# The second layer of an expert block with the weights stationary instead of the tokens

## The reference, cut to what matters

```python
def _expert_mlp(x, W1, b1, W2, b2, W3, b3):
    h = jax.nn.gelu(jnp.einsum('bnd,dh->bnh', x, W1) + b1, approximate=False)
    h = jax.nn.gelu(jnp.einsum('bnh,hk->bnk', h, W2) + b2, approximate=False)
    return jnp.einsum('bnh,hd->bnd', h, W3) + b3
...
_, topk_idx = jax.lax.top_k(scores, TOP_K)
for i in range(num_expert):
    w = jnp.mean((topk_idx == i).astype(x.dtype), axis=-1, keepdims=True)
    outputs = outputs + _expert_mlp(x, W1[i], b1[i], W2[i], b2[i], W3[i], b3[i]) * w
```

## Time and profile before

| | us |
|---|---|
| median of 3 runs | 420.71 |
| lowest and highest | 419.45, 421.0 |
| span of the profiled execution | 431.4 |

### The profile page before, as it was taken

How to read it: one execution, slowest core, us unless ns; L and a number is a source line. 1 busy time by engine, 2 the same in 40 slices (tenths; PEclk the granted TensorE clock), 3 DMA queues, 4 the chain that set the end, 5 groups by cost and what they waited for, 6 DMA issues and landing times.

```text
span 431.4 us, 7928 instructions
## 1 busy us (share of the span) xinstructions
PE 311.5 (72%) x2495; PEld 190.2 (44%) x2495; DVE 271.2 (63%) x709; ACT 183.2 (42%) x406; POOL 163.2 (38%) x185
## 2 busy tenths in 40 slices
PE   1757599999876748544999999999925275786820
PEld 1553244444343213343566666666515243564710
DVE  3587768888857233569777677767665854544513
ACT  7340147766434663402444454455382206335602
POOL 8203004134311999768055222322330472054560
PEclk9966989999998858655999999999985775696975
DMA  5689913434110456411356111010002013111114
GB/s 191 230 211 277 403 72 92 138 92 140 52 49 5 153 186 196 140 44 57 97 183 210 33 33 26 27 32 21 14 21 97 25 50 84 36 47 37 32 40 147
DMA packets 23237, 43.31 MB, mean 100 GB/s; under 512 B 3661, under 2 KB 13612, under 8 KB 23070
## 3 DMA queue, kind: packets, MB, share of 16 engines
q0 software_dynamic: 8336, 26.47, 18.9%
q1 hardware_dynamic: 13758, 13.64, 11.8%
q10 hardware_dynamic: 1104, 2.70, 1.8%
HBM read 27.25 MB, written 15.30 MB: 99 GB/s over the span
## 4 chain that ended last, share of the span: by engine, by line
PE 51%; DVE 20%; issue 8%; DMA 7%; POOL 5%; ACT 5%; another core or an unknown queue 1%; SPq 1%; ACTq 1%; POOLq 0%; DVEq 0%
PE pair L1115 14%; PE bank L1239 4%; PE bank L1012 4%; PE bank L1125 3%; PE bank L1136 3%; PE pair L970 3%; PE pair L1103 3%; DVE mA L1427 3%; PE bank L990 3%; POOL w_sb L663 2%; DMA back<-y_rows 2%; PE pair L1227 2%; POOL y_rows L733 2%; DMA y_rows<-y_sb,id_now 2%; PE bank L1004 2%
## 5 line engine op out<-in xcount | busy, mean ns | idle before, releaser
L1115 PE MATMUL pair<-w_sb,h 128*128 x276 | 64.7, 385 | 6.2 <-DVE h L1550 6.2
L1427 DVE TENSOR_REDUCE mA<-pair 128x2 f32<-128x256 f32 (+3 forms) x64 | 50.8, 821 | 16.6 <-PE pair L972 15.8
L820 ACT ACTIVATE h<-pair,cols 128x128 f32<-128x128 f32 x92 | 26.2, 368 | 79.2 <-PE pair L1103 55.9
L808 ACT ACTIVATE p_ring<-bank 128x512 f32<-128x512 f32 (+1 forms) x88 | 45.4, 563 | 32.6 <-PE bank L993 32.6
L656 POOL DMA_DIRECT2D w_ring<-in_L_ffn_W_dram x24 | 18.3, 765 | 97.4 <-DVE w_sb L1368 76.3
L717 POOL DMA_INDIRECT y_rows<-y_sb,id_now x21 | 25.0, 1190 | 70.5 <-DVE y_sb L1571 68.0
L990 PE MATMUL bank<-qr,kr 128*128 128x512 bf16 (+3 forms) x128 | 36.3, 328 | 8.8 <-ACT p_ring L808 8.6
L684 POOL DMA_INDIRECT x_slots<-sent,slot x32 | 31.8, 994 | 28.6 <-DVE slot L1670 17.1
L1115 PEld LDWEIGHTS pair<-w_sb,h 128*128 128x128 f16 x276 | 25.8, 99 | 36.3 <-issue 8.4
L970 PE MATMUL pair<-kr,qr 128*128 128x128 bf16 (+3 forms) x128 | 33.7, 320 | 7.2 <-DVE mA L1427 6.2
L820 ACT ACTIVATE h<-bank,cols 128x128 f32<-128x128 f32 x92 | 26.6, 392 | 7.2 <-PE bank L1125 7.2
(11 more groups left out here) (298 smaller groups left out, 653.2 us busy)
## 6 DMA issues: line engine op xcount, KB each, us to landing
w_ring<-in_L_ffn_W_dram POOLq DMA_DIRECT2D x24, 512.0 KB, 4.5
x_slots<-w_sb POOLq DMA_DIRECT2D x2, 2064.0 KB, 19.9
fc_sb<-in_L_ffn_c_fc_dram POOLq DMA_DIRECT2D x4, 512.0 KB
cp_sb<-in_L_ffn_c_proj_dram POOLq DMA_DIRECT2D x4, 512.0 KB
back<-y_rows SPq DMA_DIRECT2D x8, 256.0 KB, 3.3
kr<-k_rows SPq DMA_DIRECT2D x8, 204.0 KB
qr<-q_rows SPq DMA_DIRECT2D x8, 192.0 KB
x_slots<-w_sb ACTq DMA_DIRECT2D x1, 1290.0 KB, 7.2
```

The source lines that it names most:

```text
L808: act.activation(p_ring[:, w % P_RING, 0:width], bank(4 + v % 3)[:, 0:width], ACT.Exp).then_inc(exp_done, 1)
L820: ins = act.activation(to[:, c * P:(c + 1) * P], got[:, c * P:(c + 1) * P], ACT.Gelu, bias=cols[:, bass.ds(e * HC + (bias_row + c), 1)], s ...
L1115: ins = mm(bank(3), h1[:, s, hq, k * P:(k + 1) * P], w2_sb[k][wq][:, bass.ds(e * HID, HID)], start=(k == 0 and n == 0), stop=(k == HC - 1 ...
L1427: dve.tensor_reduce(mA[:, b, t, g * G + 2 * hp:g * G + 2 * hp + 2], got[:, :, 0:(t + 1) * P], AX_X, ALU.max).then_inc(a_used, 1)
```

## The change

The second layer takes the weights as the stationary operand and the activations as the moving one: for each of 4 groups of 128 output units, 4 x 3 matmuls of 128 columns. Its result has hidden units on the partitions, so Gelu reads it from PSUM at once. copy_z, transpose_z, the tile `z32` and the semaphores `z_copied` and `tz_done` go away. The result alternates between banks 3 and 4, and the second layer waits for gelu2 of two blocks before. On ACT gelu2(i) now stands ahead of gelu1(i+2); on DVE the order is the table, split_2(i), result(i-1), copy_x(i+3), split_1(i+2).

```diff
@@ -830,10 +829,10 @@
 
             def gelu2(i, e):
                 s = i % 2
-                act.wait_ge(tz_done, i + 1)
+                act.wait_ge(mm2_done, i + 1)
                 if i >= 1:
                     act.wait_ge(h2_ready, i)
-                hidden_units(i, e, bank(4), h32[:, 1], ROW_B2, gelu2_done)
+                hidden_units(i, e, bank(3 + s), h32[:, 1], ROW_B2, gelu2_done)
 
             act.activation(warm[:, 1:2], ident[:, 0:1], ACT.Gelu)
             act.wait_ge(a_used, len(a_order))
@@ -842,11 +841,11 @@
             act.wait_ge(tab_ready, 1)
             of = list(table(mybir.EngineType.Activation, 0, 0, LEAD + 2))
             for i in range(NB):
+                gelu2(i, of[i])
                 if i + 2 < NB:
                     gelu1(i + 2, of[i + 2])
                 if i + 3 < NB and i + 3 >= len(of):
                     of += table(mybir.EngineType.Activation, 0, i + 3, 1)
-                gelu2(i, of[i])
 
 
             act.wait_ge(l1w_in, 16 * (E + 1))
@@ -1108,22 +1107,15 @@
 
                 s = i % 2
                 pe.wait_ge(h1_ready, i + 1)
-                if i >= 1:
-                    pe.wait_ge(z_copied, i)
-                for k in range(HC):
-                    for n, (wq, hq) in enumerate(PRODUCTS):
-                        ins = mm(bank(3), h1[:, s, hq, k * P:(k + 1) * P], w2_sb[k][wq][:, bass.ds(e * HID, HID)],
-                                 start=(k == 0 and n == 0), stop=(k == HC - 1 and n == len(PRODUCTS) - 1))
+                if i >= 2:
+                    pe.wait_ge(gelu2_done, i - 1)
+                for m in range(HC):
+                    for k in range(HC):
+                        for n, (wq, hq) in enumerate(PRODUCTS):
+                            ins = mm(bank(3 + s)[:, m * P:(m + 1) * P],
+                                     w2_sb[k][wq][:, bass.ds(e * HID + m * P, P)], h1[:, s, hq, k * P:(k + 1) * P],
+                                     start=(k == 0 and n == 0), stop=(k == HC - 1 and n == len(PRODUCTS) - 1))
                 ins.then_inc(mm2_done, 1)
-
-            def transpose_z(i):
-
-                pe.wait_ge(z_copied, i + 1)
-                if i >= 1:
-                    pe.wait_ge(gelu2_done, i)
-                for m in range(HC):
-                    ins = tr(bank(4)[:, m * P:(m + 1) * P], z32[:, m * P:(m + 1) * P], ident[:, :])
-                ins.then_inc(tz_done, 1)
 
             def third_layer(i, e):
 
@@ -1156,7 +1148,6 @@
                     first_layer(i + 2, of[i + 2])
                 if i + 3 < NB:
                     transpose_x(i + 3)
-                transpose_z(i)
                 if i == 0:
                     low_made(pe, W_TILES - 3)
                     low_made(pe, W_TILES - 1)
@@ -1533,12 +1524,6 @@
                 copy(xgT[:, s].rearrange("p q n -> p (q n)"), bank(0).bitcast(F16)[:, 0:2 * P]
                      ).then_inc(xgT_ready, 1)
 
-            def copy_z(i):
-                dve.wait_ge(mm2_done, i + 1)
-                if i >= 1:
-                    dve.wait_ge(tz_done, i)
-                copy(z32[:, :], bank(3)).then_inc(z_copied, 1)
-
             def split_1(i):
 
                 s = i % 2
@@ -1599,16 +1584,15 @@
                     dve.wait_ge(lead_in, 16 * LEAD)
                     copy(id_all[:, LEAD - 1:LEAD], xg_lead[:, LEAD - 1, 2 * D:].bitcast(I32)).then_inc(id_copied, 1)
                     dve.wait_ge(id_copied, 1)
-                copy_z(i)
                 if i >= len(of):
                     of += table(mybir.EngineType.DVE, 0, i, 1)
+                split_2(i)
+                if i:
+                    result(i - 1, of[i - 1])
                 if i + 3 < NB:
                     copy_x(i + 3)
                 if i + 2 < NB:
                     split_1(i + 2)
-                if i:
-                    result(i - 1, of[i - 1])
-                split_2(i)
             result(NB - 1, of[NB - 1])
 
             def split_weights(e):
```

More of the change, by code:

```diff
@@ L245, in build @@
             h32 = sb("h32", [P, 2, HID], F32, f0)
-            z32 = sb("z32", [P, HID], F32, f0)
             h1 = sb("h1", [P, 2, 2, HID], F16, f0)
@@ L297, in build @@
                 "mm3_done y_ready")
-        hi1_ready, hi2_ready, z_copied, tz_done = sems("hi1_ready hi2_ready z_copied tz_done")
+        hi1_ready, hi2_ready = sems("hi1_ready hi2_ready")
         xg_in = [sem(f"xg_in{n}") for n in range(2)]
```

## The result

The changed kernel takes 453.17 us (median of 4 runs, 452.86 to 454.5), the kernel before 420.33 beside it (419.45 to 421.0): a ratio of 1.0788, with a 95% interval of 1.0757 to 1.0818. It is 33 us slower; 450 was forecast.

A forecast was written before the change was run, and what follows sets the result against it. TensorE paced the kernel before; register operations for addresses would make its sequencer pace the changed one. The terms sum to 30.1 us, scaled by 0.975 and added to the 420.71 us median: 450 us, range 418 to 458.

The forecast's parts named there:

- The mechanism: Second layer: 32 register operations for addresses instead of 8 make TensorE's sequencer pace the block, 6.3 us against 4.80; chance 0.72.
- Two of the signs: Changed kernel's profile: second-layer matmuls at a median spacing above 70 ns, and TensorE's idle time put down to issue.
- The step: TensorE's sequencer: 0.113 us from one register operation to the next; 48 take 5.4 us, with 0.9 for table and waits.
- blocks 2 to 19: The loop: 18 blocks, each 1.50 us longer, 27.0 us in all.
- blocks 20 and 21: Loop's end: block 20 without table and transposes of x, 1.0 us longer; block 21 without first layer either, 0.
- block 22's second layer: The last block's second layer: 3.6 us against 2.7, so 0.9 us longer.
- first two blocks: Start: block 0 at the low clock, paced by matmuls and gathered rows either way; block 1 loses 0.9 us net.
- from there to the last scatter's dispatch: The drain: gelu2 and split_2 before result(21), 2.3 us, against copy, transposes and third layer, 2.04: 0.3 us longer.
- The array-paced block: Rival in the loop: shorter sequencer steps leave TensorE pacing, at best 4.13 us a block, 407 us; chance 0.12 for 405 to 418.
- a step that belongs to the profiling: Sequencer: steps shorter where no profile is taken, so a 6.3 us loop in the profile but no longer time; no separate chance.
- Shared addresses: Rival in the second layer: the four m of a tile share address steps, 8 operations as now, 407 us; chance 0.04.
- weight loads: Second layer: four times as many loads cost 0 to 0.17 us a block, 0 taken; as rival, 4.4 us, no forecast change.

The follow-up runs named there:

- the kernels with 32 and 48 operations: 32 a block: the changed kernel with only the low halves of the second layer's weights read at expert 0, 413.46 us; 48 a block: the changed kernel, 453.17 us.
- second execution: The kernel before run once more with no edit, for another profile: 420.91 us, span 419.1.
- the long first execution: The kernel before, unedited, in the profiled execution that the prediction rests on: span 431.4 us, against timed runs of 419.5 to 421.
- all three executions of before: The kernel before, unedited, profiled three times: spans 431.4, 419.1 and 417.5 us; the two repeats measured 420.91 and 419.29 us.
- the kernel with fixed addresses: The changed kernel with the second layer always reading expert 0's weights, so no register operations there: 408.25 us, ratio to before 0.9687.
- both grouped ones: The changed kernel with register operations issued several to an instruction: in the second layer alone, 415.71 us; in all three layers, 402.77 us.
- the cut one: The kernel before with only its second layer cut into 48 matmuls of 128 columns, activations still stationary: 461.44 us, ratio 1.0951.

## Why the prediction was right, and where it was off

**The mechanism held.** 32 register operations where there were 8; taking them away gives 408 us, adding them to the old form without the rest of the change costs 41.6 us, issuing the same ones in 8 instructions brings the second layer back to 2.85 us, and to 2.68 once the first and third layers' are grouped too. Clock 1.00, VectorE's share of the loop down to 43%, the order of work worth nothing at this block: as forecast. Two of the signs fitted badly. The median spacing of the second layer's matmuls is 58 ns and not above 70, because in a three two steps are 55 to 58 ns and one is 113; the mean is 79. And TensorE's idle time hardly shows as issue (7 of 119 us), because the records cover it.

**The step was mis-sized: 6.30 us a block forecast, 6.64 measured.** 0.113 us is the median of the steps, and 616 of 713 steps between neighbouring address instructions of the second layer in the trace have it. Nearly all others, 86, take 0.13 to 0.27, 0.18 on average, and of those that follow another in the same second layer 58 of 63 come 32 or 33 instructions after it, counting matmuls, weight loads and register operations. The mean step is 0.120, the slope between the kernels with 32 and 48 operations 0.119: 48 x 0.119 is 5.7 us where the forecast had 5.4, and that is the missing 0.3. The stretches of the earlier trace rows, 8 steps at most, were too short to show the late ones.

**The sum, term by term**, as the difference of the starts and ends in the trace of the changed kernel and of the kernel before in its second execution:

| term | forecast, us | measured, us |
|---|---|---|
| blocks 2 to 19 | 27.0 | 119.45 - 86.65 = 32.8 |
| blocks 20 and 21 | 1.0 | 11.03 - 9.57 = 1.5 |
| block 22's second layer | 0.9 | 3.79 - 2.37 = 1.4 |
| first two blocks | 0.9 | 15.21 - 16.06 = -0.9 |
| from there to the last scatter's dispatch | 0.3 | 7.06 - 7.77 = -0.7 |
| sum | 30.1 | 34.1 |
| stretches that the change doesn't touch | none | -2.1 |
| span | 30.1 | 451.1 - 419.1 = 32.0 |

The loop was 5.8 us dearer than forecast, the ends 2 us cheaper, and it is partly luck that the result came within 3.2 us of 450. The first two blocks show where I was wrong the other way (TensorE in order of time, blocks 0 and 2 of the changed kernel, then of before):

```profile
194.39 3.86 PE L1115 MATMUL pair<-h,w_sb 128*128 128x128 f16 x48 [2.17 <-DVE h L1535]
...
209.60 3.91 PE L1115 MATMUL pair<-h,w_sb 128*128 128x128 f16 x48
```
```profile
195.64 2.76 PE L1115 MATMUL pair<-w_sb,h 128*128 x12 [2.46 <-DVE h L1550]
...
211.70 2.75 PE L1115 MATMUL pair<-w_sb,h 128*128 x12
```

Block 0 to block 1 is 9.04 us against 10.45, and 9.0 to 9.1 in every kernel without the copy and the transposes of z, 10.3 to 10.5 in the others but the long first execution (6.1, where block 0 began 8 us later): their removal is worth 1.4 us there, which I had set to nothing. Before block 1 TensorE waits 3.6 us for the copy of z in the kernel before and transposes after it, and 3.5 us for the last weights (L1359) in the changed one. The low clock that I gave to block 0 belongs to the long execution (0.65 there); in the two others shown here block 0 ran at 1.00, and block 1 at 0.72 after and 0.84 before. At the drain, result(21)'s scatter is dispatched 3.7 us after the last second-layer matmul starts in both (343.87 to 347.57 and 310.29 to 313.98), so the 0.3 of the longer way didn't appear; the last dispatch then waits for the landing of the one before it, 3.4 us on instead of 4.1.

**The scaling was wrong.** I multiplied the sum by 0.975 because the profiled execution was 10.7 us over the median, as if the loop were shorter by that share in a usual run. The loop is the same in all three executions of before. That took 0.8 us off.

**Hidden work.** "Every block costs the sequencer 6.3 us, so it can't get ahead" held, but the other side of the same model, that its 3.65 us hide wholly behind 4.80 of matmuls, did not: 0.1 us a block showed in the kernel before, 0.35 with no operations in the second layer, 0.6 with its operations grouped. Hiding needs a lead at the right place, and the lead has a bound: some 17 matmuls, which are 2.69 us of wide ones but 0.93 of narrow ones.

**The rivals.** The array-paced block was priced rightly, 4.13 us, 407 us in all: 4.15 and 402.8 were reached once the addresses were grouped, so that rival named what the change would be worth without its side effect. Its reason for being likely, that the long execution's excess might sit in the steps, fell: the excess lay outside the loop. Nothing speaks for a step that belongs to the profiling: all four timed runs are longer by as much as the profile's loop. But the profile shown is of one of them, and no run is on record as taken without the profiler, so this isn't settled. Shared addresses didn't occur (32 operations). For weight loads I took 0 out of 0 to 0.17; 48 narrow matmuls take 2.68 us where the 12 wide ones take 2.59 with grouped addresses, so the narrow form, loads included, costs 0.09.

## What to carry to other kernels

Count what the sequencer issues, not only what the engine computes: here an address made from a register cost an instruction for each distinct slice, and cutting an operand into four turned 8 of them into 32, which alone cost 41.6 us (461.4 - 419.8) where the removed transposes and copy were worth 10. The sign is a row of matmuls that got longer as a whole while each record stayed as short and the engine still reads as busy; the cure was to keep the change and group the address operations, which made it 17 us faster than before. Whether sequencer work hides is read where it falls behind (after a table read, at a layer with few matmuls per address), not from its sum over a block; and narrow matmuls make the time in which it can hide shorter.

## What the runs showed of the hardware

- Register operations cost TensorE's sequencer by the instruction: 0.113 us for one operation, 0.124 for three in one instruction, 0.138 for six.
- At the table read the sequencer was never further ahead of TensorE than 17 matmuls with their weight loads: 0.93 us where they are narrow, in each of the loop's 18 blocks, in the kernel with fixed addresses and in both grouped ones; up to 2.69 us where 12 of them have 512 columns (the kernel before with grouped addresses).
- About every 32nd instruction of TensorE's stream came late in the second layer of the changed kernel and of the cut one, by 0.06 us on average. What makes it late is open: no run varied it.
- Two executions of one kernel differ by up to 9 us at the start of block 0 (3.7 at that of block 2) and by 10 us behind the last scatter, while the loop agrees to 0.2 us; a single profile's span is no scale for its stages.
